# Aggregates, value products and mask products cut to tiles of 64 rows of TensorE in a fused four-layer graph kernel

## What is computed

```python
x = _layernorm(x + _L0_gnn_ref(x, W, a, beta, adj))    # graph attention: softmax over nodes, then att @ h
x = _layernorm(x + _L1_gnn_ref(x, adj, weight, bias))  # y = einsum('nm,bmd->bnd', adj, x); y @ weight + bias
x = _layernorm(x + _L2_gnn_ref(x, w_qkv, ..., adj))    # 8 heads of 32: softmax(where(adj == 0, -inf, q k^T)) @ v
x = _layernorm(x + _L3_gnn_ref(x, adj, adj, ...))      # 3 steps of a gated unit:
#   a  = einsum('nm,bmd->bnd', adj, h)                 # "aggregate"
#   z, r = sigmoid(a.. + h..);  hv = tanh(a.. + (r * h)..);  h = (1 - z) * h + z * hv
```

## Time and profile before

| | |
|---|---|
| time, median of 3 runs (lowest to highest) | 1490.12 us (1485.84 to 1490.32) |
| time of the profiled execution | 1490.44 us |
| its span in the profile | 1488.4 us |
| TensorE matmul busy (PE) | 1367.9 us (92%) |
| TensorE weight load busy (PEld) | 1155.1 us (78%) |
| VectorE busy (DVE) | 1058.9 us (71%) |
| ScalarE busy (ACT) | 794.4 us (53%) |
| GpSimd busy (POOL) | 146.4 us (10%) |

### The profile page before, as it was taken

How to read it: one execution, slowest core, us unless ns; L and a number is a source line. 1 busy time by engine, 2 the same in 40 slices (tenths; PEclk the granted TensorE clock), 3 DMA queues, 4 the chain that set the end, 5 groups by cost and what they waited for, 6 DMA issues and landing times.

```text
span 1488.4 us, 26652 instructions
## 1 busy us (share of the span) xinstructions
PE 1367.9 (92%) x10357; PEld 1155.1 (78%) x10357; DVE 1058.9 (71%) x2366; ACT 794.4 (53%) x1450; POOL 146.4 (10%) x196
## 2 busy tenths in 40 slices
PE   3465899999999999999999999999999999998895
PEld 2455688888888888888888888888888888877674
DVE  3545487777778787778778787778778787757533
ACT  1342455565656555665656565665656565645342
POOL 4200001110001001110001000110001010101000
PEclk9678899999999999999999999999999999999887
DMA  4000100000000000001000000001000000000000
GB/s 136 15 22 1 36 2 22 29 15 24 14 21 28 21 28 21 28 14 35 7 14 28 21 28 21 28 14 35 14 7 28 22 29 8 30 8 29 1 29 15
DMA packets 54662, 34.62 MB, mean 23 GB/s; under 512 B 34897, under 2 KB 51537, under 8 KB 54609
## 3 DMA queue, kind: packets, MB, share of 16 engines
q1 hardware_dynamic: 52800, 29.43, 6.6%
q0 software_dynamic: 1248, 3.94, 0.8%
q10 hardware_dynamic: 560, 0.52, 0.1%
HBM read 12.92 MB, written 8.39 MB: 14 GB/s over the span
## 4 chain that ended last, share of the span: by engine, by line
PE 67%; DVE 17%; ACT 8%; issue 4%; POOL 2%; DMA 0%; ACTq 0%; SPq 0%; POOLq 0%; DVEq 0%
PE banks L109 15%; PE banks L111 15%; PE banks L110 15%; PE banks L485 7%; PE banks L480 3%; PE banks L537 2%; PE banks L629 2%; PE banks L614 2%; ACT y L284 2%; PE banks L603 2%; DVE l_stats L256 2%; DVE l_r L1399 1%; ACT banks L982 1%; DVE late_lo L1148 1%; ACT l_qk L908 1%
## 5 line engine op out<-in xcount | busy, mean ns | idle before, releaser
L971 ACT ACTIVATE l_r<-banks,bias_r 128x512 f32<-128x512 f32 x96 | 65.9, 686 | 223.8 <-PE banks L111 223.8
L270 POOL TENSOR_TENSOR l_rstd<-l_mv,eps 128x4 f32<-128x4 f32 x48 | 28.2, 587 | 949.4 <-DVE l_mv L264 949.4
L988 ACT ACTIVATE banks<-banks,bias_h 128x512 f32<-128x512 f32 x96 | 63.3, 659 | 60.6 <-PE banks L111 60.5
L1148 DVE TENSOR_TENSOR l_rh_lo<-l_r,l_rh_hi 128x512 fp32r<-128x512 f32 x96 | 66.1, 688 | 37.0 <-ACT l_rh_hi L847 36.7
L1399 DVE SCALAR_TENSOR_TENSOR l_r<-banks,l_r 128x512 f32<-128x512 f32 x96 | 66.1, 688 | 32.0 <-ACT banks L982 29.2
L1381 DVE SCALAR_TENSOR_TENSOR l_r<-l_r,l_h 128x512 f32<-128x512 f32 x64 | 43.6, 682 | 54.9 <-ACT l_r L971 54.9
L284 ACT ACTIVATE y<-l_sum,l_offset,l_rstd 128x256 f32<-128x256 f32 x128 | 70.6, 591 | 19.1 <-DVE l_offset L278 19.1
L485 PE MATMUL banks<-adj_t,y 128*128 128x128 f32 x512 | 68.6, 285 | 11.3 <-ACT y L284 9.9
L109 PE MATMUL banks<-l_rh_hi,u_hi 128*128 128x512 f32 x192 | 78.2, 407 | 0.0
L982 ACT ACTIVATE banks<-banks,bias_z 128x512 f32<-128x512 f32 x96 | 63.4, 661 | 25.9 <-PE banks L111 25.9
L110 PE MATMUL banks<-l_rh_lo,u_hi 128*128 128x512 f32 x192 | 75.7, 394 | 0.0
(11 more groups left out here) (238 smaller groups left out, 4366.3 us busy)
## 6 DMA issues: line engine op xcount, KB each, us to landing
x_tok<-in_x_dram SPq DMA_DIRECT2D x16, 512.0 KB, 3.8
l_res<-y SPq DMA_DIRECT2D x16, 512.0 KB, 2.9
out_dram<-l_res SPq DMA_DIRECT2D x16, 512.0 KB, 2.9
l_vpair<-l_vstage SPq DMA_DIRECT2D x32, 128.0 KB, 3.2
w_raw<-in_L_gnn_w_w_dram POOLq DMA_DIRECT2D x3, 512.0 KB, 9.9
qkv_raw<-in_L_gnn_w_qkv_dram POOLq DMA_DIRECT2D x1, 768.0 KB, 7.7
u_raw<-in_L_gnn_u_w_dram POOLq DMA_DIRECT2D x2, 256.0 KB, 9.7
l_w_raw<-in_L_gnn_W_dram ACTq DMA_DIRECT2D x1, 256.0 KB, 5.0
```

What stands on the lines that cost most here:

```text
L971: nc.scalar.activation(b.r[:, m, :], RZ[:, m, :], ACT.Tanh, scale=0.5, bias=w.biases["r"][:, m:m + 1]).then_inc(s.r_ready.sem, 1)
L988: nc.scalar.activation(HV[:, m, :], HV[:, m, :], ACT.Tanh, bias=w.biases["h"][:, m:m + 1]).then_inc(s.hv_ready.sem, 1)
L1148: return nc.vector.tensor_tensor(parts[1][:, k, :], bank, parts[0][:, k, :].bitcast(F32), ALU.subtract)
```

## The change

Three groups of products are cut so that each matmul uses 64 rows of the array (64 partitions of its operands).

- *Aggregates*: in place of one matmul with the block-diagonal `adj_t` there are two for each tile and half, one for each graph: 64 rows by 128 columns by 64. Graph n's results go into bank n of the pair, both halves k side by side, not into bank k. So `adj_done` and its like are signalled for both banks only by the last two matmuls of the second call (k = 1, t = 3). The copies behind it (`l1_high`, `l3_high_a`, `f_high_a` and the `low` ones) take a bank by graph and write both halves in pieces of 64.
- *Value products*: in place of one matmul with two heads there are two, one for each head e, of 64 rows by 64 columns by 33; head e goes into bank e of a pair of banks, so two tiles share two banks. `v_pair` loses its zeros (`VW` from 66 to 33), and the first matmul of tile t = 0 or 2 waits for the copies of two tiles' probabilities. An increment of a semaphore that nobody waits for (`l2_attending`) stands there too.
- *Mask products*: the stationary operand is the 64-row identity twice side by side, and banks 0 and 2 use rows 0 to 63, banks 1 and 3 rows 64 to 127.

The core of the diff:

```diff
-        def aggregate(bank, tokens, k):
+        def aggregate(banks, tokens, k, done):
             for t in range(TILES):
-                ins = nc.tensor.matmul(bank[:, columns(t)], tokens[:, t, k * P:(k + 1) * P], p.adj_t[:, :],
-                                       start=True, stop=True)
-            return ins
+                for n in range(PER_TILE):
+                    q = slice(n * NODES, (n + 1) * NODES)
+                    at = (k * TILES + t) * NODES
+                    ins = nc.tensor.matmul(banks[:, n, at:at + NODES], tokens[q, t, k * P:(k + 1) * P],
+                                           p.adj_t[q, q], start=True, stop=True)
+                    if (k, t) == (CH - 1, TILES - 1):
+                        ins.then_inc(done.sem, 1)
...
             for r in range(ROWS):
-                nc.tensor.matmul(Y[:, r, :], p.ident_bf[:, :],
-                                 p.mask_bias[:, :].unsqueeze(1).to_broadcast([P, TILES * CH, NODES]),
+                q = slice((r % 2) * NODES, (r % 2 + 1) * NODES)
+                nc.tensor.matmul(Y[:, r, :], p.ident2_bf[q, :, :].rearrange("p b j -> p (b j)"),
+                                 p.mask_bias[q, :].unsqueeze(1).to_broadcast([NODES, TILES * CH, NODES]),
                                  start=True, stop=False, skip_group_check=True)
...
-            pe.wait_ge(*s.l2_prob_t.at(u, t + 1))
+            if t % 2 == 0:
+                pe.wait_ge(*s.l2_prob_t.at(u, t + 2))
+                pe.sem_inc(s.l2_attending, 1)
             for g in range(HP):
                 for n in range(PER_TILE):
-                    at = g * P + n * NODES
-                    ins = nc.tensor.matmul(Y[n * NODES:(n + 1) * NODES, t, g * VW:(g + 1) * VW],
-                                           probt[:, t, at:at + NODES], b.v_pair[:, n, t, g, :],
-                                           start=True, stop=True)
+                    for e in range(2):
+                        q = slice(e * NODES, (e + 1) * NODES)
+                        at = g * P + n * NODES
+                        col = ((t % 2) * HP + g) * VW
+                        ins = nc.tensor.matmul(Y[n * NODES:(n + 1) * NODES, t // 2 * 2 + e, col:col + VW],
+                                               probt[q, t, at:at + NODES], b.v_pair[q, n, t, g, :],
+                                               start=True, stop=True)
...
-        def l1_high(u, k):
-            act.wait_ge(*s.l1_adj_done.at(u, k + 1))
-            copy(b.late[0][:, k, :], Y[:, k, :]).then_inc(s.l1_hi.sem, 1)
+        def l1_high(u, n):
+            act.wait_ge(*s.l1_adj_done.at(u, n + 1))
+            copy(of_graphs(b.late[0], n), by_tile(Y[:, n, :])).then_inc(s.l1_hi.sem, 1)
...
-        def l3_high_a(u, step, k):
-            act.wait_ge(*s.adj_done.at(u, CH * step + k + 1))
-            copy(b.l3_as[0][:, k, :], HV[:, k, :]).then_inc(s.a_hi.sem, 1)
+        def l3_high_a(u, step, n):
+            act.wait_ge(*s.adj_done.at(u, CH * step + n + 1))
+            copy(of_graphs(b.l3_as[0], n), by_tile(HV[:, n, :])).then_inc(s.a_hi.sem, 1)
```

More of the change, by code:

```diff
@@ L22 @@
 HP = HEADS // 2
-VW = 2 * HD + 2
+VW = HD + 1
 QK_BANK = (2, 3, 0, 1)
@@ L167, in _ @@
             nc.vector.memset(p.same_graph[q, q], 1.0)
-        nc.vector.tensor_copy(p.ident_bf[:, :], p.ident[:, :])
-        nc.vector.tensor_tensor(p.ident2[:, :], p.ident[:, 0:NODES], p.ident[:, NODES:P], ALU.add)
+        links.link(nc.vector.tensor_tensor(p.ident2[:, :], p.ident[:, 0:NODES], p.ident[:, NODES:P], ALU.add))
+        for b in range(PER_TILE):
+            nc.vector.tensor_copy(p.ident2_bf[:, b, :], p.ident2[:, :])
         nc.vector.tensor_scalar(p.mask_bias[:, :], p.adj2[:, :], 0.0, MASKED, ALU.is_equal, ALU.mult)
@@ L382, in pair_of, with of_graphs, by_tile @@
         return slice(2 * n, 2 * n + 2)
+    def of_graphs(parts, n):
+        return parts.rearrange("p k (t n i) -> p n k t i", t=TILES, n=PER_TILE)[:, n, :, :, :]
+    def by_tile(bank):
+        return bank.rearrange("p (k t i) -> p k t i", k=CH, t=TILES)
     def columns(t):
@@ L411, in l2_swap @@
                 there = slice((1 - n) * NODES, (2 - n) * NODES)
-                sp.dma_start(b.v_pair[there, n, :, :, (1 - n) * HD:(2 - n) * HD],
+                sp.dma_start(b.v_pair[there, n, :, :, 0:HD],
                              b.v_stage[here, :, :, :]).then_inc(s.l2_v_swapped.sem, 16)
@@ L544, in l1_aggregate @@
                 past(pe, s.l2_proj, u - 1, 2)
-            aggregate(Y[:, k, :], b.y0, k).then_inc(s.l1_adj_done.sem, 1)
+            aggregate(Y[:, 0:2, :], b.y0, k, s.l1_adj_done)
         @within
@@ L914, in l2_take_v @@
                 act.wait_ge(*s.l2_v_done.at(u, 1))
-                if isinstance(u, int) and u == 0:
-                    act.wait_ge(s.blank, 1)
             q = slice(n * NODES, (n + 1) * NODES)
@@ L921, in l2_take_v @@
             else:
-                copy(b.v_pair[q, n, :, :, n * HD:(n + 1) * HD], values[:, :, :, n, :])
+                copy(b.v_pair[q, n, :, :, 0:HD], values[:, :, :, n, :])
         @within
@@ L962, in f_high_a @@
         @within
-        def f_high_a(u, k):
-            act.wait_ge(*s.f_adj_done.at(u, k + 1))
+        def f_high_a(u, n):
+            act.wait_ge(*s.f_adj_done.at(u, n + 1))
             past(act, s.h_new, u - 1, CH)
-            copy(b.f_as[0][:, k, :], Y[:, 2 + k, :]).then_inc(s.f_a_hi.sem, 1)
+            copy(of_graphs(b.f_as[0], n), by_tile(Y[:, 2 + n, :])).then_inc(s.f_a_hi.sem, 1)
         @within
@@ L1119, in split_attention @@
             dve.wait_ge(w.loaded[2], 80)
-            dve.wait_ge(s.blank, 1)
-            for e in range(2):
-                q = slice(e * NODES, (e + 1) * NODES)
-                nc.vector.memset(b.v_pair[q, :, :, :, 2 * HD + e], 1.0).then_inc(s.ones, 1)
+            nc.vector.memset(b.v_pair[:, :, :, :, HD], 1.0).then_inc(s.ones, 1)
             dve.wait_ge(ws["l1_hi"], 1)
@@ L1148, in lower, with lower_of_graphs @@
             return nc.vector.tensor_tensor(parts[1][:, k, :], bank, parts[0][:, k, :].bitcast(F32), ALU.subtract)
+        def lower_of_graphs(parts, n, bank):
+            return nc.vector.tensor_tensor(of_graphs(parts[1], n), by_tile(bank), of_graphs(parts[0], n).bitcast(F32),
+                                           ALU.subtract)
         def over_tiles(row, n):
@@ L1259, in l1_low @@
         @within
-        def l1_low(u, k):
-            dve.wait_ge(*s.l1_hi.at(u, k + 1))
-            lower(b.late, k, Y[:, k, :]).then_inc(s.l1_lo.sem, 1)
+        def l1_low(u, n):
+            dve.wait_ge(*s.l1_hi.at(u, n + 1))
+            lower_of_graphs(b.late, n, Y[:, n, :]).then_inc(s.l1_lo.sem, 1)
         @within
@@ L1315, in l2_share @@
                 dve.wait_ge(*s.l2_inv.at(u, 2))
-            ins = nc.vector.tensor_tensor(b.o_tok[:, t, :].rearrange("p (g e d) -> p g e d", g=HP, e=2),
-                                          heads[:, t, :, 0:2 * HD].rearrange("p g (e d) -> p g e d", e=2),
-                                          b.inv[:, t, :, :].unsqueeze(3).to_broadcast([P, HP, 2, HD]), ALU.mult)
+            banks, at = pair_of(t // 2), slice((t % 2) * HP, (t % 2 + 1) * HP)
+            ins = nc.vector.tensor_tensor(b.o_tok[:, t, :].rearrange("p (g e d) -> p e g d", g=HP, e=2),
+                                          heads[:, banks, at, 0:HD],
+                                          b.inv[:, banks, at].unsqueeze(3).to_broadcast([P, 2, HP, HD]), ALU.mult)
             if t == TILES - 1:
@@ L1370, in f_low_a @@
         @within
-        def f_low_a(u, k):
-            dve.wait_ge(*s.f_a_hi.at(u, k + 1))
-            lower(b.f_as, k, Y[:, 2 + k, :]).then_inc(s.f_a_lo.sem, 1)
+        def f_low_a(u, n):
+            dve.wait_ge(*s.f_a_hi.at(u, n + 1))
+            lower_of_graphs(b.f_as, n, Y[:, 2 + n, :]).then_inc(s.f_a_lo.sem, 1)
         def h_before(step):
@@ L1413, in l3_low_a @@
         @within
-        def l3_low_a(u, step, k):
-            dve.wait_ge(*s.a_hi.at(u, CH * step + k + 1))
-            lower(b.l3_as, k, HV[:, k, :]).then_inc(s.a_lo.sem, 1)
+        def l3_low_a(u, step, n):
+            dve.wait_ge(*s.a_hi.at(u, CH * step + n + 1))
+            lower_of_graphs(b.l3_as, n, HV[:, n, :]).then_inc(s.a_lo.sem, 1)
         @within
```

19 lines of the change are left out of this document (9 added, 10 removed).

## The result

| | before | after |
|---|---|---|
| time, median (lowest to highest) | 1488.91 us (1485.84 to 1490.32, 4 runs) | 1504.95 us (1503.23 to 1508.39, 4 runs) |
| time of the profiled execution | 1490.44 us | 1503.43 us |
| span | 1488.4 us | 1501.4 us |

The ratio is 1.0099, with a 95% interval of 1.0079 to 1.0118: slower by 1%. The medians differ by 16.0 us and the profiled executions by 13.0, where 6.1 were forecast.

What follows compares the result with a forecast made beforehand. TensorE was taken to set the pace, waiting a little each round for ScalarE and VectorE. Place A's stall in 14 rounds, plus B, C and mask in 16, gave +6.1 us: 1496.5 us, range 1478 to 1510 (forecast's own 1491 to 1503).

Steps and rivals of the forecast that it cites:

- rival 4: The mask doesn't halve, or the value products run at their upper bound: +7 or +3, 1500 to 1504 us (8%).
- A pair takes what one matmul took: Aggregates: two side-by-side matmuls take about 0.109 us, limited by the 128-column load, where one full matmul took 0.111.
- Rivals 2 and 3: Aggregates: 2, loads go with rows, half the time, 1458 us (8%); 3, loads unhidden or taking turns, 1544 us (6%).
- The switch in rows: Between 128x128 and 64x128 tiles: 0.09 to 0.10 us of nothing, then the load of 0.10, no longer hidden.
- Rival 1: A switch in rows is free: B and C gain 0.04 us each, A's stall stays, 1489.7 us (20%).
- Place A: At l3_aggregate, later copies stall VectorE 0.53 us in each of 14 rounds; TensorE's own 0.06 lies within it.
- Places B and C: Two other places of aggregates, 16 pairs each: +0.25 us at B and +0.10 at C in each of 16 rounds.
- Mask: Mask product: four matmuls run two and two side by side, -0.43 us a round; the switch hides in waiting.
- Value products, copies in pieces of 64: Value products 0, set by loads of 64 columns (bounds -0.4 and +0.2 us); copies in smaller pieces 0.
- The sum: All terms: 14 x 0.53 + 16 x (0.25 + 0.10 - 0.43) = +6.1 us on the profiled 1490.44.
- the clock is full: Step ahead of the per-round terms: all were reckoned at full clock, as granted (1.00) in the steady part.

Runs made afterwards that it cites:

- e3: The changed kernel with each aggregate matmul, except the last two of each pair of calls, streaming its 64 columns twice (128): 1498.52 us, ratio 1.0049.
- e4: The changed kernel with each aggregate matmul cut into two of 64 weight columns (tiles of 64x64): 1511.6 us, ratio 1.0139.
- e1: The changed kernel with one call moved in ScalarE's list, l1_high(i + 2, 0) behind the second l3_high_a: 1498.73 us, ratio 1.0051.
- e5: The kernel before with only the mask product in two tiles of 64 rows: 1479.26 us, ratio 0.9939.
- e6: The kernel before with mask and value products in tiles of 64 rows, aggregates as before: 1485.36 us, ratio 0.9963.

## Why the prediction came out as it did

The direction and the mechanisms held. The size of the sum was too small by half: +6.1 us forecast, +13.0 measured in the profiled executions. The median of 1504.95 us lies above the forecast's own range (1491 to 1503). That it lies within 1478 to 1510 is luck in part, since the room above 1503 was made for rival 4, which is not what happened.

- *A pair takes what one matmul took.* Held: 0.109 forecast, 0.111 measured, and e3 and e4 show that it is the load's columns (128 columns streamed instead of 64: no change; 64 weight columns instead of 128: 0.06). The prediction's parts of the 0.109, 0.104 and 5 ns, stand in no row; only their sum was measured. Rivals 2 and 3 are refuted. The Trainium skill (TensorEngine Tiling, Theoretical Speedup and Performance Considerations) recommends two row tiles for a contraction of 64, for up to twice the speed; the trace disagrees for these fp32 products, and agrees for the mask, whose four matmuls stream 512 columns each behind their loads.
- *The switch in rows.* Held: 0.10 us and 0.11 of unhidden load at C, forecast as 0.09 and 0.10, now from a switch that changes rows alone. Rival 1 is refuted. The Trainium skill's rule that a change of tiling mode drains TensorE (TensorEngine Tiling, Key Properties) agrees.
- *Place A.* Held, and in its mechanism shown by e1. The second `l_a_lo` was forecast 0.53 to 0.54 us late; by the same reckoning, from start to start, it is 0.60 late (the 0.54 in its row is only the idle time ahead of it), and a round loses 0.62. The copy that holds it up waits for all of A, and 31 pairs at 0.111 instead of 0.109 are 0.06 of the difference. TensorE alone leaves A 0.17 later, not 0.06; that is hidden, as forecast.
- *Places B and C.* Mis-sized, +0.33 and +0.14 for +0.25 and +0.10. Fifteen steps of 0.002 explain 0.03 in each; 0.05 of B and 0.01 of C stay unexplained.
- *Mask.* Held: -0.43 forecast, -0.42 alone (e5), -0.37 beside the rest.
- *Value products, copies in pieces of 64.* Held: 0.00 (e6), and no copy became longer.
- *The sum.* With the measured terms it is 14 x 0.62 + 16 x (0.33 + 0.14 - 0.37 - 0.05 - 0.07) = +8.4 us instead of +6.1. The other 4.6 of the profiled 13.0 were no term at all: the step "the clock is full" left out the ends. One pause of 1.5 us stands in code that is written out behind the loop and runs for the first time, in the value products' new form (e6 has it too, the kernels with the old form don't). From the last mask to the end it is 3.0 us, by estimate 1 of work and 2 of a lower granted clock. The clock at the ends moves the time of the kernels by several us, in either direction, with nearly the same work in them: behind the last mask it is 135.4 to 143.8 us at 0.95 to 0.89, while length times clock stays at 127 to 129. What decides it stays open, and no run here changed it alone.

## What to carry to other kernels

Before cutting a matmul into row tiles, compare the columns that it streams with those that it loads. In these traces what streamed longer than its load gained from rows (the mask), what was bound by its load did not (aggregates and value products), and the aggregates gained from fewer weight columns for each tile. When a result moves to banks that are finished together, look at the in-order queue of every engine that reads them: one copy ahead of another in ScalarE's list cost 0.62 us a round, more than the tiles themselves. And before adding matmuls to a loop, count what it already holds, and look at the packets of the queue of instructions in one round afterwards, and at the granted clock behind each pause.
